# Cross-attention kernel: one ring of seven PSUM banks, an order of work for each engine, and row maxima on four 32-row strips

## The reference

```python
x = x + _L0_xattn_ref(_layernorm(x), ctx, ctx, mask, Wq, bq, Wk, bk, Wv, bv, Wo, bo)
x = x + _L0_ffn_ref(_layernorm(x), w1, w2)

# attention
q = split_heads(query @ Wq + bq); k = split_heads(key @ Wk + bk); v = split_heads(value @ Wv + bv)
scores = einsum('bhqd,bhkd->bhqk', q, k) / sqrt(8)
scores = where(mask == 0, -1e9, scores)          # mask: (32, 1, 56, 1500)
out = einsum('bhqk,bhkd->bhqd', softmax(scores), v) @ Wo + bo
# feed-forward: activations quantised to 8 bits by row, weights to -1, 0, 1
h = gelu(bitlinear(x, w1)); return bitlinear(h, w2)
```

## Time and profile before

| | |
|---|---|
| median of 3 runs | 1424.34 us (1422.21 to 1429.65) |
| the profiled execution: time, span | 1425.48 us, 1423.7 us |
| PE / DVE / ACT / POOL busy | 1134.3 (80%) / 801.5 (56%) / 646.3 (45%) / 111.2 us (8%) |
| mean granted TensorE clock | 0.911 of full speed |

### The profile page before, as it was taken

The page is one execution under the profiler, slowest core; times in us unless marked ns, Lnnn a source line. Parts: engine busy times, 40 slices in busy tenths (PEclk is TensorE's granted clock), DMA queues, the critical chain, the costliest instruction groups (busy, mean ns, idle before and its releaser), DMA issues.

```text
span 1423.7 us, 32699 instructions
## 1 busy us (share of the span) xinstructions
PE 1134.3 (80%) x11716; PEld 780.0 (55%) x11716; DVE 801.5 (56%) x2689; ACT 646.3 (45%) x1176; POOL 111.2 (8%) x156
## 2 busy tenths in 40 slices
PE   5777888878788887888878788887888878788875
PEld 3455555555555655555555555655555555555553
DVE  5755556545565564556546466564556546466552
ACT  2244454444544444444444444444444444444452
POOL 4001000000000000000000000000000000000000
PEclk8798999989899898999989899998999989899997
DMA  6201111101111011111101111011111101110000
GB/s 140 74 3 41 42 43 43 32 10 41 41 42 41 20 27 37 42 41 42 35 8 40 41 42 41 22 25 35 42 41 42 37 5 40 41 42 0 2 2 4
DMA packets 59374, 49.34 MB, mean 35 GB/s; under 512 B 2784, under 2 KB 55632, under 8 KB 59344
## 3 DMA queue, kind: packets, MB, share of 16 engines
q1 hardware_dynamic: 57551, 48.11, 12.8%
q10 hardware_dynamic: 1793, 0.83, 0.2%
HBM read 47.91 MB, written 0.92 MB: 34 GB/s over the span
## 4 chain that ended last, share of the span: by engine, by line
PE 56%; DVE 19%; ACT 13%; issue 10%; DMA 1%; DVEq 1%; ACTq 0%; SPq 0%
PE ps_s L722 20%; PE ps_v L757 10%; PE ps_p L661 10%; PE ps_p L669 7%; DVE max_junk L930 6%; ACT probs L572 4%; ACT mask_sum_junk L536 3%; PE ps_p L657 3%; PE ps_p L654 3%; DVE k_lo L915 2%; ACT k_hi L558 2%; DVE recip L965 2%; ACT L572 1%; ACT L555 1%; DMA ctx_sb<-in_ctx_dram 1%
## 5 line engine op out<-in xcount | busy, mean ns | idle before, releaser
L572 ACT ACTIVATE probs<-ps_s 125x448 f32<-125x448 f32 x768 | 375.9, 541 | 553.5 <-PE ps_s L722 553.3
L930 DVE CUSTOM_DVE_ANT_0 max_junk<-ps_p,mask_bias 120x500 bf16<-120x500 f32 x768 | 474.2, 674 | 74.3 <-PE ps_p L669 65.5
L669 PE MATMUL ps_p<-k_hi,qry_hi 64*120 64x500 f32 x768 | 231.4, 469 | 110.8 <-DVE k_lo L915 90.1
L722 PE MATMUL ps_s<-qry_hi,k_hi 64*125 64x448 f32 x768 | 215.9, 472 | 22.7 <-ACT probs L572 22.6
L669 PEld LDWEIGHTS ps_p<-k_hi,qry_hi 64*120 64x120 f32 x768 | 97.6, 183 | 245.7 <-DVE k_lo L915 113.9
L915 DVE SCALAR_TENSOR_TENSOR k_lo<-ps_p,bk_sb,k_hi 128x500 fp32r<-128x500 f32 x96 | 70.8, 738 | 199.0 <-ACT k_hi L558 196.7
L757 PE MATMUL ps_v<-probs,vals 125*32 125x112 f32 x6144 | 177.4, 270 | 1.2 <-ACT probs L572 1.2
L722 PE MATMUL ps_s<-own_query,mask_bias 57*125 57x448 f32 x768 | 175.2, 387 | 0.8 <-DMA own_query<-shift 0.8
L722 PE MATMUL ps_s<-qry_hi,k_lo 64*125 64x448 f32 x768 | 174.8, 388 | 0.0
L722 PE MATMUL ps_s<-qry_lo,k_hi 64*125 64x448 f32 x768 | 173.0, 383 | 0.0
L757 PEld LDWEIGHTS ps_v<-probs,vals 125*32 125x32 f32 x6144 | 154.1, 115 | 17.4 <-issue 10.4
(11 more groups left out here) (122 smaller groups left out, 863.9 us busy)
## 6 DMA issues: line engine op xcount, KB each, us to landing
ctx_sb<-in_ctx_dram SPq DMA_DIRECT2D x31, 750.0 KB
mask_sb<-in_mask_Bx1xSxS_ik_dram SPq DMA_DIRECT2D x64, 328.1 KB
own_query<-shift SPq DMA_DIRECT2D x64, 1.8 KB
out_dram<-x_rows SPq DMA_DIRECT2D x16, 56.0 KB, 1.6
ctx_sb<-in_ctx_dram ACTq DMA_DIRECT2D x1, 750.0 KB
x_rows<-in_x_dram SPq DMA_DIRECT2D x1, 672.0 KB, 10.6
w_sb<-in_L_ffn_w_dram SPq DMA_DIRECT2D x2, 256.0 KB, 8.7
x_rows<-in_x_dram SPq DMA_DIRECT2D x1, 224.0 KB, 5.2
```

The lines of the kernel that those rows point to most:

```text
L572: act.activation(probs[:, c % NP, h], ps_s[0:KC, j % NS, 0:HC], ACT.Exp).then_inc(exp_done, 1)
L669: mm = pe.matmul(bank[0:MROWS, 0:SEG], qry_hi[rows, p, a:a + 2, :].rearrange("p a q -> p (a q)")[:, 0:MROWS], k_hi[rows, p, s * SEG:(s + 1 ...
L722: mm = pe.matmul(ps_s[0:KC, (2 * c + h) % NS, 0:HC].rearrange("k (a q) -> k a q", a=HH), key[part, :], query[part], start=(n == 0), stop=( ...
L930: dve.tensor_tensor_reduce(max_junk[0:MROWS, BANK[how][slot], :], bank[0:MROWS, 0:SEG], mask_bias[0:MROWS, p, s * SEG:(s + 1) * SEG].bitca ...
```

## The change

PSUM: the three score banks and the four of the ring become one ring of seven (`NBANK = 7`). A score chunk takes two slots of the ring, one for each half, and a group of maxima takes four.

Order: instead of one list for all engines there is one for each of PE, ACT, DVE and POOL (`PE_EVEN`, `ACT_EVEN` and so on).

Keys: ACT copies the biased projection whole into SBUF (`kf`, `k_full`, two buffers), which releases the bank. A second ACT copy rounds it (`kh`, `k_hi`), and GpSimd subtracts (`kl`, `k_lo`). DVE has no part in it.

Maxima: six groups of four matmuls a batch, each matmul with 32 contraction rows, on four row strips of the array and into four banks. Their number, columns and readers stay the same. `some_diag` is widened to 128 rows with zeros, and some feed-forward buffers now lie in weight buffers that are no longer needed.

```diff
-TAKEN_BY_DVE = "kFMRQZWDBOHUY"
-COUNT = {"T": 3, "K": 3, "F": 1, "V": 3, "M": NM, "R": 1, "D": 1}
+TAKEN_BY_DVE = "FRQZWDBOHUY"
+TAKEN_BY_ACT = "TVXG"
+COUNT = {"T": 3, "K": 3, "F": 1, "V": 3, "R": 1, "D": 1}
+WIDTH = {"S": 2, "s": 2, "M": 4}
+NBANK = 7
...
-    own s0 T0 T1 D0 f0 M0 M1 M2 M3 S1 V0 O0 S2 T2 M4 M5 M6 M7 S3 rows S4 K0 k0 M8 M9 M10 M11 S5 V1 bias0
+    T0 V0 T1 M0 K0 D0 s0 f0 S1 S2 S3 M1 S4 S5 S6 M2 O0 K1 T2 S7 S8 S9 S10 M3 P0 M4 P1 M5 S11 V1 K2 F0 V2 R0 P2
...
+            def low_keys(bt, n):
+
+                b, k, p = bt
+                at = slice(n * SEG, (n + 1) * SEG)
+                pool.wait_ge(k_hi_ready, NSEG * b + n + 1)
+                pool.tensor_tensor(k_lo[:, p, at], k_full[:, (p + n) % 2, :], k_hi[:, p, at].bitcast(F32), ALU.subtract)\
+                    .then_inc(k_lo_ready, 1)
...
-                elif kind == "K":
-                    wait(act, scores_ready, NC * (b - 2) + NG * (n + 1))
-                    act.activation(k_hi[:, p, n * SEG:(n + 1) * SEG], bank[:, 0:SEG], ACT.Identity,
-                                   bias=bk_sb[:, 0:1]).then_inc(k_hi_ready, 1)
...
+            def full_keys(slot, how, st):
...
+                wait_bank_full(act, ("K", n, 0), how, st)
+                wait(act, k_lo_ready, NSEG * b + n - 1)
+                act.activation(k_full[:, (p + n) % 2, :], ps_p[:, BANK[how]["K", n, 0], 0:SEG], ACT.Identity,
+                               bias=bk_sb[:, 0:1]).then_inc(k_full_ready, 1)
...
+            def high_keys(slot, st):
...
+                act.wait_ge(k_full_ready, NSEG * b + n + 1)
+                wait(act, scores_ready, NC * (b - 2) + NG * (n + 1))
+                act.activation(k_hi[:, p, at], k_full[:, (p + n) % 2, :], ACT.Copy).then_inc(k_hi_ready, 1)
...
+            def maxima(slot, how, st):
...
+                for h in range(4):
+                    wait_bank_free(pe, ("M", n, h), how, st)
+                for h in range(4):
+                    rows, a = slice(32 * h, 32 * (h + 1)), 4 * (h % 2) + 2 * r
+                    pe.matmul(ps_p[0:MROWS, BANK[how]["M", n, h], 0:SEG],
+                              qry_hi[rows, p, a:a + 2, :].rearrange("p a q -> p (a q)")[:, 0:MROWS],
+                              k_hi[rows, p, s * SEG:(s + 1) * SEG], start=True, stop=True)\
+                        .then_inc(bank_full[BANK[how]["M", n, h]], 1)
...
-                if kind == "k":
-                    dve.wait_ge(k_hi_ready, NSEG * b + n + 1)
-                    at = slice(n * SEG, (n + 1) * SEG)
-                    dve.scalar_tensor_tensor(out=k_lo[:, p, at], in0=bank[:, 0:SEG], scalar=bk_sb[:, 0:1],
-                                             in1=k_hi[:, p, at].bitcast(F32), op0=ALU.add, op1=ALU.subtract)\
-                        .then_inc(k_lo_ready, 1)
```

More of the change, by code:

```diff
@@ L103, with bank_slots @@
+POOL_PASS = passes("kl0 q0 kl1 kl2", "kl0 q0 kl1 kl2", POOL_EVEN, POOL_ODD, "", {}, {"%s%d" % POOL_ODD[0]: "fold"})
 PREVIOUS = {"lead": "open", "first_even": "lead", "first_odd": "first_even", "even": "odd", "odd": "even",
             "last_even": "odd", "last_odd": "last_even", "tail": "last_odd"}
-NBANK = 4
-NS = 3
-NG = 4
-NP = NC
-FLAT = {how: [s for s in PASS[how] if s[0] in BANKED] for how in PASS}
+def bank_slots(slots):
+    return [("S" if kind == "s" else kind, n, part) for kind, n in slots
+            if kind in BANKED or kind in WIDTH for part in range(WIDTH.get(kind, 1))]
@@ L457, in _ @@
             put(pool.memset(ones_f[:], 1.0))
+            put(pool.memset(some_diag[:], 0.0))
             pool.tensor_copy(ones_bf[:], ones_f[:]).then_inc(consts, 1)
@@ L608, in fill @@
                 t = pair_of(st)
[L609 removed]
+                bank = ps_p[:, BANK[how][kind, n, 0], :]
                 if kind == "X":
```

284 lines of the change are left out of this document (161 added, 123 removed).

## The result

The changed kernel takes **1010.4 us** (median of 4 runs, 1009.1 to 1013.5), against 1426.99 us (1422.2 to 1430.5) for the kernel before on the same chip: a ratio of 0.7085 [0.7055, 0.7115]. The forecast was 1090 us with a range of 1025 to 1235. The direction was right; the size was not, and the range does not hold the result.

A forecast was written before the change was run, and what follows sets the result against it. TensorE was taken as the bound, losing time to waits of order and slow work behind them. 58 us work plus 6 waiting made 64 a pair for 85.34; 299 saved in 14 pairs, 334 altogether: 1090 us, range 1025 to 1235.

The forecast's parts named there:

- What bounds the kernel: TensorE, busy 80% of the span, loses time to waits of order behind DVE and ACT and to half-speed work afterwards.
- Work, 58 us: TensorE's busy time per pair of passes after the change: priced matmuls and split changes sum to 52.1, times 1.12.
- a factor of 1.12: Observed TensorE work of 65 us a pair over the 57.9 priced for the old order, applied to the new order too.
- Waits, 6 us: TensorE's waiting per pair after the change: 4.6 us laid out slot by slot, made 6 for hand-overs rounded away.
- The hand layout: Both new passes laid out with prices and the seven-bank rule: they end at 29.7 and 29.2 us, waits 4.6.
- the forecast 35: Savings outside the 14 looped pairs: 16 us each for the first and last pair, 3 for the lead.
- no loss beyond the layout: Rival: a pair of passes takes 59 us, the whole kernel under 1020 us; chance 0.04.
- Strips: Maxima matmuls on four 32-row strips overlap fully: 0.22 us a group for 0.44, saving 2.6 us a pair.
- Clock: Without 3 us waits TensorE runs near 1.00 in the loop, and 5 us of slow work a pair vanish.
- The rival that it stays low: Waits of about 3 us before maxima groups keep TensorE's work at 1.2 GHz: slower than before, 1550 us; chance 0.05.
- Ring: Slacks of only 0.3 us at many places; rival that bank waits grow: pair 70 to 80 us, 1175 to 1340, chance 0.20.
- Moved to others: Key work shifted between engines costs nothing beside TensorE: ACT 44, DVE 43, GpSimd 13 us of a 64 us pair.

The follow-up runs named there:

- the last run of it: Kernel before with mask sum early, the change's key path, and DVE reading only 125 of 500 columns of each maxima bank: 1178.6 us, ratio 0.8281.

## Why the prediction was wrong, and what in it was right

**What bounds the kernel: right.** Removing the late mask sum alone gave 146 us, the key path behind it 53. Along this one path the rest is: ring and strips in the old order 23 (1225.6 to 1202.4), and the remaining orders 192 (1202.4 to 1010.4). By another path the shares are others (mechanisms first: 108, then the sum's place 114, then the orders 192), but the orders are more than half on both. Both paths build the ring before the last step of the orders, and one bank less costs 101 of that step's 192 us, so orders and ring are not two gains that simply add up. No run took the old order's chunks and waits apart any further.

**Work, 58 us: this step failed.** The step is "Sum 57.9, against 65 observed, a factor of 1.12 for what my list lacks", and then "52.1, times 1.12". The new kernel is busy 54.5 us a pair, and 52.9 where DVE does not hold it, so the list of 52.1 was nearly right without a factor. What the factor stood for belonged to the kernel before. By the timeline of the last run of it:

- Groups whose fourth matmul is held up for its bank count as busy, and the chunk behind runs with its halves out of step. The twelve groups take 9.9 us and the chunks behind them about 13.4 (the slow one counted as 1.12), where the list has 12 x 1.44 = 17.3 us for both: 6 us.
- Work at the low clock behind the one wait that was left: 0.98 + 0.68 = 1.7 us. The pairs without it are busy 1.5 us less.

57.9 + 6.0 + 1.7 = 65.6, against 64.8 busy. In the changed kernel both are gone: a group asks for its four banks before its first matmul, starts all four within 0.01 us, and no wait in the loop is followed by a lower clock. The list itself was right for group and chunk, 1.44 for the 1.47 measured on 64 rows. The account is from rows, and the 1.47 is from another order and ring; no run of the kernel before lets its groups wait for four banks at once. Also, the 65 was read from windows in which TensorE waited, and "busy" there was taken for work.

**Waits, 6 us: too many.** They are 3.3. The hand layout had 4.6; the 1.4 that I added for rounding were not there. The layout's two passes, 58.9 us, came within 2% of the 57.8 measured. Without their waits they hold 54.3 us of work, close to the 54.5 busy, while the sum of the same prices gave 52.1: the two did not agree, and the forecast went by the second and its factor. Of the 6.2 us by which the pair was over-forecast, the factor is 3.5 and the waits 2.7; fourteen pairs make 86 us. The ends gave 31 for the forecast 35. The rival "no loss beyond the layout" is what happened, and 0.04 was too little for it: the factor and the rounding both pushed the same way, and the bottom of the range rested on both.

**Strips: the size right, the effect not.** A group takes 0.43 us to the next split (0.22 and 0.20 for the change of split were priced), and 0.65 on halves (0.44 and 0.20). But strips bring nothing measurable in this kernel (1010.4 and 1012.2, with the collision unlike in the two), and 8 us once the mask bias is moved. The Trainium skill (TensorE: Matmul & The Clock Gate; Measured speedup vs the span model) gives four strips 3.07 times. By it the saving of a group over halves would be an estimated 0.16 us; the runs show 0.22, which is what full overlap gives.

**Clock: right.** All 14 looped pairs have 1.00, and waits of up to 0.7 us did no harm. The rival that it stays low did not come.

**Ring: right that it has little slack.** The waits left are for it, none over 0.8 us in the pair shown, and one bank less costs 10%.

**Moved to others: right for ACT and in the loads of all three** (41.6, 46.6 and 13.3 us for 44, 43 and 13), wrong in what they do to the path. DVE's loss of six `k_lo` was counted as worth nothing beside TensorE. With them back on DVE and the stall gone the kernel is 40 us slower, but mostly because the query blocks then fall on another operation of DVE. And "under 1 us a pair ... and DVE has 20 us of slack" took DVE's slack over the pair for cover. Two of the six in a pair are hit, for 1.1 and 0.9 us, where a fifth were to be, for 0.5 to 0.8. The mask biases lose 96 x (738 - 460) ns = 27 us in the whole kernel, 2.0 a looped pair, and 10 us of it reaches the end, because at that place eleven maxima run back to back behind the operation and TensorE waits for their banks. The Trainium skill (SBUF — State Buffer; SBUF: two separate sides) says that a DVE operation in a two-port mode, or with two SBUF inputs, and one of GpSimd shut each other out for a whole instruction. The trace agrees for the mask bias, if it is in such a mode: 0.42 us become 1.51 beside a subtraction of 1.25.

## What to carry to other kernels

Before building new buffers for an engine that waits, look at what stands in the queue ahead of what it waits for: here one slot without inputs of its own, moved ahead in its pass, gave 10%, and orders gave more than half of 29%, with a ring of seven banks to stand on. A factor between a price list and an observed busy time must be explained row by row before it is carried to another order, since part of it can be waiting that counts as busy, or work out of step behind such a wait. Average slack of an engine covers nothing at the place where a queue of short work stands behind one long instruction, so price a collision at its place in the order. And look at the profile page's loads of instructions before blaming a slot for a stall at the turn of a loop.
